# A two-layer recurrent block on one core: the feed-forward's hidden activations in two buffers, its input's split on POOL, its norm two chunks ahead, and another order at its start and at the kernel's end

## The chip, the cores and the metric

The kernel runs on one core of a Trainium2 chip. The metric is the device time of one execution in microseconds. The engines are TensorE (PE in the profile, PEld its weight loads), VectorE (DVE), ScalarE (ACT), GpSimd (POOL) and SyncE (SP), which issues every DMA here. Each engine runs its own list of instructions in order and waits on semaphores for the others.

## What is computed

Four sequences of 1024 tokens, 128 channels. The input is layer-normalised to `xn`. One branch is a block attention on `xn` (16 heads of 8, blocks of 32). The other has two layers of windowed attention and feed-forward. The output is `x + attention * silu(branch)`.

```python
def _layer(x, wqkv, qs, ksc, wo, lg, lb, w1, b1, w2, b2):
    h = shift_token(x)                      # half of the channels come from the token before
    q, k, v = split(h @ wqkv)               # 8 heads of 64, q and k normalised, rotated
    x = x + local_attention(q, k, v) @ wo   # windows of 64, each sees itself and the one before
    h = shift_token(x)
    mu = h.mean(-1, keepdims=True)
    var = h.var(-1, keepdims=True)
    h = (h - mu) / jnp.sqrt(var + 1e-05) * lg + lb
    h = h @ w1 + b1
    a, g = jnp.split(h, 2, axis=-1)         # 341 and 341 columns
    h = a * jax.nn.gelu(g, approximate=False)
    return x + h @ w2 + b2

xn = _layernorm(x)
s = _L0_attn_ref(xn, ...)
for l in range(2): y = _layer(y, ...)       # y starts as xn
out = x + s * silu(y)
```

## The kernel before

Everything lies in SBUF with channels on the partitions; `X` holds all 4096 tokens. The order of each engine is written out by hand, so program order is the schedule. The first phase (to about 165 us) is the input norm and the block attention. Then each of two layers, L0 and L1, has a windowed attention over 32 tiles of 128 tokens (`local(n)` on each engine, tile `n`'s parts spread over several calls), and a feed-forward over 8 chunks of 512 tokens (`ffn(j)` on each engine).

The feed-forward of chunk j is a chain through all engines. PE makes the column mean of the shifted `x` (`mean`, one fp32 matmul), DVE subtracts it (`centre`, writes `D`), ACT squares (`squares`), PE makes the variance (`variance`, one fp32 matmul), ACT takes Ln and Exp(-0.5 ·) (`inverse_deviation`), DVE scales (`scaled`, writes `tA`). The result is split into a high and a low part for three single-pass matmuls: ACT copies it to `split[.., 0, :]` (L954, L972), DVE subtracts that (`lows`, L1253). PE then makes, for each of three parts c of the hidden layer, the gate side and the linear side, 3 matmuls each (`up(c)`: PSUM banks 1 to 6). ACT applies Gelu to the gate side (L949), DVE adds the bias to the linear side and multiplies (`hidden(c)`, L1262, writes `hid`, which lies in the attention's `prob`). PE multiplies by `w2` (three fp32 matmuls into bank 7, the down projection), DVE adds it to `X` (L1274), SP copies the chunk to the shifted buffer `XS` for the next layer.

Before the change `ffn(j)` runs chunk j's `up`, chunk j-1's down projection at the end of the same step, and the norm of chunk j+3. There is one `hid`, so `hidden(0)` of a chunk waits until the down projection of the chunk before is done. On DVE `hidden` of chunk j-1 stands in `ffn(j)`, behind `lows(j+1)`. Gelu, Ln/Exp and Silu need different function tables in ACT, so each step has two table loads, and with L1's Silu in it four. The last layer ends each chunk with Silu (L959), a multiply with the attention's result (L1285) and an add of the input (L1288) on DVE, and a DMA of the chunk.

Between attention and feed-forward, the attention's last tiles (`local(31)` to `local(34)` in the PE list) come first, with the means and variances of chunks 0, 1 and 2 between them; the split of `w1` (L1106, L1108) also stands there on DVE. POOL does nothing in the feed-forward. In the attention it normalises probabilities (L1375) and rotates q and k (L1382 to L1404).

L422 and L432 are the helpers through which every matmul and every transpose goes.

## Time and profile before

| | us |
|---|---|
| median of three runs | 882.16 (880.42 to 882.94) |
| the profiled execution | 883.38 |
| its span, first to last instruction | 881.6 |
| PE busy in it | 787.1 (89%) |
| DVE busy | 682.5 (77%) |
| ACT busy | 669.7 (76%) |
| POOL busy | 531.5 (60%) |
| TensorE clock granted, mean | 0.954 of full |

A time is read against the same execution's span: 1.78 us lie around it. The stages in this span: block attention to about 165 us, L0's windowed attention to about 420, its feed-forward to about 520, L1's windowed attention to about 764, its feed-forward and the output to the end. In the timeline rows a time is a start, the next number a duration, and a bracket tells how long the engine had been idle before and what ended that.

### The profile page before, as it was taken

How to read it: one execution, taken by the hardware profiler on the slowest of the kernel's cores; microseconds unless marked ns; L12 is line 12 of the kernel's file. 1: busy time of each engine (PE TensorE's matmuls, PEld its weight loads, DVE VectorE, ACT ScalarE, POOL GpSimd, SP SyncE). 2: the span in 40 equal slices, each digit the busy share in tenths (PEclk: the TensorE clock that was granted, in tenths of full speed). 3: DMA queues.
4: the chain of work that ended last, by engine and by line, in shares of the span. 5: the costliest groups of instructions: out<-in, count | busy, mean ns of one | idle time of the engine just before them, and what ended most of it. 6: DMA issues, size and time to landing. Idle time of an engine off the chain costs nothing. (4 is left out here: it accounts for less than half of the span.)

```text
span 881.6 us, 26513 instructions
## 1 busy us (share of the span) xinstructions
PE 787.1 (89%) x9720; PEld 595.3 (68%) x9720; DVE 682.5 (77%) x1338; ACT 669.7 (76%) x2041; POOL 531.5 (60%) x505
## 2 busy tenths in 40 slices
PE   4788999878999999999779887999999999878985
PEld 1457777656888888887645545788888888654542
DVE  1577899789999999996234669999999999524455
ACT  2326777549999999998577526999999999747873
POOL 0364334169999999999200007999999999710000
PEclk8899999969999999999899988999999999989996
DMA  9120001002222222222101112222222222212001
GB/s 317 43 49 3 3 4 42 3 19 52 65 65 64 65 64 66 65 65 65 45 19 25 27 34 61 53 65 64 66 65 65 64 65 65 65 31 95 1 36 60
DMA packets 64707, 48.26 MB, mean 55 GB/s; under 512 B 40410, under 2 KB 50948, under 8 KB 64068
## 3 DMA queue, kind: packets, MB, share of 16 engines
q1 hardware_dynamic: 64580, 46.57, 20.9%
...
## 5 line engine op out<-in xcount | busy, mean ns | idle before, releaser
L422 PE MATMUL ps<-wqkv,split 128*128 128x512 f32 x576 | 188.5, 438 | 20.3 <-DVE tA L1157 13.4
L899 ACT ACTIVATE prob<-ps,nmax 128x128 f32<-128x128 f32 x512 | 179.3, 375 | 2.7 <-DVE nmax L1196 2.7
L1382 POOL TENSOR_TENSOR qr<-qr,ss 128x512 f32<-128x512 f32 x64 | 92.0, 1437 | 118.3 <-ACT ss L892 118.3
L1375 POOL TENSOR_TENSOR prob<-prob,rinv 128x512 f32<-128x512 f32 x128 | 133.2, 1042 | 29.1 <-DVE rinv L1203 28.9
L422 PEld LDWEIGHTS ps<-wqkv,split 128*128 128x128 f32 x576 | 98.7, 198 | 35.1 <-issue 25.0
L899 ACT ACTIVATION_READ_ACCUMULATOR prob<-ps,nmax 128x1 f32 x512 | 110.5, 216 | 0.0
L432 PE MATMUL ps<-ident,prob 128*128 128x128 f32 x640 | 97.2, 275 | 9.5 <-POOL prob L1375 9.2
L422 PE MATMUL ps<-split,w 128*128 128x512 f32 (+1 forms) x288 | 87.7, 447 | 15.9 <-DVE prob L1262 14.2
L1196 DVE TENSOR_REDUCE nmax<-ps 128x4 f32<-128x512 f32 x128 | 81.6, 677 | 11.8 <-PE ps L422 11.5
L432 PEld LDWEIGHTS ps<-ident,prob 128*128 128x128 f32 x640 | 76.0, 141 | 21.2 <-POOL prob L1375 13.0
L867 ACT ACTIVATE pT<-ps 128x512 f32<-128x512 f32 x128 | 80.7, 631 | 11.3 <-PE ps L432 11.1
L1390 POOL TENSOR_TENSOR kA<-kn,lrot 128x512 f32<-128x512 f32 x64 | 84.2, 1316 | 0.9 <-DVE kn L1189 0.9
L422 PEld LDWEIGHTS ps<-split,w 128*128 128x128 f32 (+1 forms) x288 | 51.4, 183 | 48.4 <-DVE prob L1262 20.4
L1404 POOL TENSOR_TENSOR kr<-kA,kB 128x512 f32<-128x512 f32 x64 | 81.8, 1277 | 0.3
L422 PE MATMUL ps<-oT,wo 128*128 128x128 f32 x512 | 76.7, 294 | 0.9 <-DVE X L1210 0.9
L1356 POOL TENSOR_TENSOR prob<-D,hmask 128x512 f32<-128x512 f32 x32 | 35.1, 1098 | 59.7 <-PE ps L422 59.6
L422 PE MATMUL ps<-pT,VB 128*64 128x64 f32 x1024 | 67.7, 231 | 3.4 <-issue 3.4
L422 PEld LDWEIGHTS ps<-pT,VB 128*64 128x64 f32 x1024 | 53.1, 140 | 25.8 <-issue 25.8
L422 PEld LDWEIGHTS ps<-oT,wo 128*128 128x128 f32 x512 | 64.3, 197 | 5.8 <-issue 1.5
L422 PE MATMUL ps<-kT,qT 64*64 64x128 f32 x2048 | 67.7, 271 | 0.0
L422 PE MATMUL ps<-pT,V 128*64 128x64 f32 x1024 | 64.7, 225 | 0.0
L422 PEld LDWEIGHTS ps<-kT,qT 64*64 64x64 f32 x2048 | 61.1, 134 | 4.7 <-issue 0.2
(128 smaller groups left out, 1871.8 us busy)
## 6 DMA issues: line engine op xcount, KB each, us to landing
...
XS<-X SPq DMA_DIRECT2D x128, 32.0 KB, 1.9
...
```

The costliest lines, as they stand in the source:

```text
L422: return nc.tensor.matmul(o, l, r, start=start, stop=stop, skip_group_check=True)
L432: return nc.tensor.matmul(o, i, ident[:], is_transpose=True, start=True, stop=True, skip_group_check=True)
L867: nc.scalar.activation(pT[:, grp, :], ps[:, 6, :], ACT.Copy).then_inc(l_pTe[grp], 1)
L899: nc.scalar.activation(prob[:, m % 2, grp, s * P:(s + 1) * P], ps[:, 4 + grp, s * P:(s + 1) * P], ACT.Exp, bias=nmax[:, m % 2, col], accum ...
L1196: v.tensor_reduce(nmax[:, m % 2, 4 * grp:4 * grp + 4], ps[:, 4 + grp, :].rearrange("p (s k) -> p s k", s=4), AX_X, ALU.max, negate=True).t ...
L1356: g.tensor_tensor(kexp[:, par, :].rearrange("p (b h k) -> p b h k", b=BLKS, h=INGRP), part(kR, n, P).rearrange("p (b k) -> p b k", b=BLKS) ...
L1375: g.tensor_tensor(p4, p4, rinv[:, m % 2, 4 * grp:4 * grp + 4].unsqueeze(2).broadcast_to([P, 4, P]), ALU.mult).then_inc(l_prob[grp], 1)
L1382: g.tensor_tensor(hd(qr[:, m % 2, :]), hd(qr[:, m % 2, :]), ss[:, (base + m) % 2, 0:8].unsqueeze(2).broadcast_to([P, HEADS, HD]), ALU.mult ...
L1390: g.tensor_tensor(hd(kA[:]), hd(kn[:]), row8(2, m, 0, HD), ALU.mult)
L1404: g.tensor_tensor(kr[:, m % 2, :], kA[:], kB[:], ALU.add).then_inc(l_kr, 1)
```

## The change

- The hidden activations have two buffers: parts 0 and 1 of chunk j in `prob[:, j % 2]`, part 2 in a slice of `vexp`. The waits for the down projection go one chunk further back.
- The high and low parts of the normalised input are made on POOL (`norm_high`, `norm_low`) from `tA` and `tB` in turn. The copy on ACT and the subtraction on DVE are gone.
- The norm runs two chunks ahead, all in bank 0. A step is on PE `mean(j+2)`, `up(j,0)`, `variance(j+2)`, `down(j-1)`, `up(j,1)`, `up(j,2)`; the three `hidden` of chunk j stand in step j.
- The change-over from attention to feed-forward is written out: the last four tiles' operations and chunk 0's steps are interleaved. `w1`'s split moves into the attention, around `local(20)`.
- L1's Silus stand in two batches, five between chunk 6 and chunk 7 and the rest behind chunk 7. POOL does multiply and add for chunks 0 to 4, DVE for 5 to 7, and chunk 7's last steps run in two halves of 256 columns, the second down projection into bank 0.
- In L0 the tables for L1 (`attn_tables`) stand ahead of `ffn(5)` on DVE, the split of the next `wqkv` ahead of `ffn(6)`.

```diff
@@ -293,6 +296,10 @@
 
         def part(t, j, width):
             return t[:, bass.ds(j * width, width)]
+
+        def hid(j, c):
+
+            return prob[:, j % 2, c, :] if c < 2 else hidx[:, j % 2, :]
 
...
+                def down(j, cols=slice(0, CHUNK), bank=7):
+                    wait(pe, x_new, x_before_ffn(L) + j)
+                    if bank == 0:
+                        pe.wait_ge(ln_log, nb + CHUNKS)
+                    for c, (u, n) in enumerate(PARTS):
+                        pe.wait_ge(ffn_hid, NPART * (fb + j) + c + 1)
+                        last = mm(ps[:, bank, cols], w2[0:n, c, :], hid(j, c)[0:n, cols], c == 0, c == NPART - 1)
+                    last.then_inc(ffn_y, 1)
+
+                def ffn(j):
+                    if j + 2 < CHUNKS:
+                        mean(j + 2)
+                    pe.wait_ge(ffn_lo, fb + j + 1)
+                    up(j, 0)
+                    if j + 2 < CHUNKS:
+                        variance(j + 2)
+                    down(j - 1)
+                    up(j, 1)
+                    up(j, 2)
 
...
+                mean(0)
+                local(TILES - 2, 0)
+                variance(0)
+                local(TILES - 1, 1)
+                mean(1)
+                local(TILES, 0)
+                variance(1)
-                local(TILES, 0)
-                bias_products()
+                pe.wait_ge(w1_made, 1 + L)
+                pe.wait_ge(ffn_lo, fb + 1)
+                up(0, 0)
                 local(TILES + 1, 1)
+                mean(2)
                 local(TILES + 2, 0)
-                variance(2, 2, 0)
                 pe.wait_ge(bias_made, 1 + L)
-                steps(0, CHUNKS - 1 if L + 1 < DEPTH else CHUNKS, ffn)
-                return ffn
+                up(0, 1)
+                variance(2)
+                pe.wait_ge(l_exp[1], 4 * (base + TILES))
+                pe.wait_ge(l_pTe[0], base + TILES)
+                pe.wait_ge(l_pTe[1], base + TILES)
+                up(0, 2)
+                for j in range(1, CHUNKS):
+                    ffn(j)
+                if L + 1 == DEPTH:
+                    for h in range(2):
+                        down(CHUNKS - 1, slice(h * CHUNK // 2, (h + 1) * CHUNK // 2), (7, 0)[h])
+
+                def last_down(j, par):
+                    down(CHUNKS - 1)
+                return last_down
 
...
+                def ffn(j):
+                    if j + 2 < CHUNKS:
+                        squares(j + 2)
+                    gelu(j, 0)
+                    if j + 2 < CHUNKS:
+                        load_exp_and_ln()
+                        inverse_deviation(j + 2)
+                    gelu(j, 1)
+                    gelu(j, 2)
+
+                def silu(j, cols):
+                    x = X[:, bass.ds(j * CHUNK + cols.start, cols.stop - cols.start)]
+                    nc.scalar.activation(x, x, ACT.Silu).then_inc(gate_silu, 1)
+
+                squares(0)
+                local(TILES - 2, 0)
+                probs_copied(TILES - 3, 1)
                 act.wait_ge(l_trq, base + TILES)
-                for j in range(3):
-                    inverse_deviation(j, j)
-                for j, t in enumerate((tA, tB)):
-                    act.wait_ge(ln_scaled, fb + j + 1)
-                    nc.scalar.activation(split[:, j, 0, :], t[:], ACT.Copy).then_inc(ffn_hi, 1)
+                inverse_deviation(0)
+                exponentials(TILES - 1, 0)
+                exponentials(TILES - 1, 1)
+                probs_copied(TILES - 2, 0)
+                o_copied(TILES - 3)
+                probs_copied(TILES - 2, 1)
+                squares(1)
+                probs_copied(TILES - 1, 0)
+                o_copied(TILES - 2)
+                inverse_deviation(1)
                 act.wait_ge(bias_made, 1 + L)
-                if L + 1 < DEPTH:
-                    steps(0, CHUNKS - 1, ffn)
-                else:
-                    steps(0, CHUNKS + 2, ffn)
+                gelu(0, 0)
+                probs_copied(TILES - 1, 1)
+                o_copied(TILES - 1)
+                squares(2)
+                load_exp_and_ln()
+                inverse_deviation(2)
+                gelu(0, 1)
+                gelu(0, 2)
+                for j in range(1, CHUNKS):
+                    ffn(j)
+                    if L + 1 == DEPTH and j == CHUNKS - 2:
+                        for k in range(GATE_POOL):
+                            act.wait_ge(x_new, x_before_ffn(L) + k + 1)
+                            silu(k, slice(0, CHUNK))
+                if L + 1 == DEPTH:
+                    for k in range(GATE_POOL, CHUNKS - 1):
+                        act.wait_ge(x_new, x_before_ffn(L) + k + 1)
+                        silu(k, slice(0, CHUNK))
+                    for h in range(2):
+                        act.wait_ge(x_new, x_before_ffn(L) + CHUNKS + h)
+                        silu(CHUNKS - 1, slice(h * CHUNK // 2, (h + 1) * CHUNK // 2))
 
...
-                steps(0, TILES - 2, local)
+                steps(0, 19, local)
+                ffn_weights_hi(L)
+                local(20, 0)
+                ffn_weights_lo(L)
+                steps(21, TILES - 3, local)
 
...
+                def ffn(j):
+                    if j + 2 < CHUNKS:
+                        norm_centre(j + 2)
+                    hidden(j, 0)
+                    summed(j - 1)
+                    if j + 2 < CHUNKS:
+                        scaled(j + 2)
+                    hidden(j, 1)
+                    hidden(j, 2)
+
+                norm_centre(0)
+                local(TILES - 2, 0)
+                inverse_sums(TILES - 3, 1)
+                inverse_sums(TILES - 2, 0)
+                inverse_sums(TILES - 2, 1)
+                v_copied(TILES - 1)
+                maxima(TILES - 1, 0)
+                maxima(TILES - 1, 1)
+                scaled(0)
+                added_to_x(TILES - 4)
+                inverse_sums(TILES - 1, 0)
+                norm_centre(1)
+                inverse_sums(TILES - 1, 1)
+                added_to_x(TILES - 3)
                 ffn_bias(L)
-                local(TILES + 1, 1)
-
-                def scaled(j, t):
-                    dve.wait_ge(ln_rstd, nb + j + 1)
-                    v.tensor_tensor(t[:], part(D, j, CHUNK), rstd[:, j, :], ALU.mult).then_inc(ln_scaled, 1)
-
-                local(TILES + 2, 0)
-                scaled(0, tA)
-                scaled(1, tB)
-                lows(0, 0, tA)
-                lows(1, 1, tB)
-                dve.wait_ge(bias_made, 1 + L)
-                if L + 1 < DEPTH:
-                    steps(0, CHUNKS - 3, ffn)
-
-                    attn_tables(L + 1, 0)
-                    attn_tables(L + 1, 1)
-                    ffn(CHUNKS - 2, 0)
-                    attn_hi(L + 1)
-                    attn_lo(L + 1)
-                    ffn(CHUNKS - 1, 1)
-                else:
-                    for j in range(CHUNKS + 4):
-                        ffn(j, j % 2)
-                return ffn
+                scaled(1)
+                hidden(0, 0)
+                added_to_x(TILES - 2)
+                norm_centre(2)
+                added_to_x(TILES - 1)
+                scaled(2)
+                hidden(0, 1)
+                hidden(0, 2)
+                for j in range(1, CHUNKS):
+                    if not gate and j == CHUNKS - 3:
+                        attn_tables(L + 1, 0)
+                        attn_tables(L + 1, 1)
+                    if not gate and j == CHUNKS - 2:
+                        attn_hi(L + 1)
+                        attn_lo(L + 1)
+                    ffn(j)
+                if gate:
+                    for k in range(GATE_POOL, CHUNKS - 2):
+                        gated(k, slice(0, CHUNK), k)
+                    gated(CHUNKS - 2, slice(0, CHUNK), CHUNKS - 2)
+                    for h in range(2):
+                        cols = slice(h * CHUNK // 2, (h + 1) * CHUNK // 2)
+                        summed(CHUNKS - 1, cols, (7, 0)[h], h)
+                        gated(CHUNKS - 1, cols, CHUNKS - 1 + h)
+
+                def tail(j, par):
+                    if j == CHUNKS + 1:
+                        summed(CHUNKS - 1)
+                return tail
...
+
+                fb = L * CHUNKS
+
+                def norm_high(j):
+                    pool.wait_ge(ln_scaled, fb + j + 1)
+                    wait(pool, ffn_a, (NPART * (fb + j - 1)) if j > 1 else 0)
+                    g.tensor_copy(split[:, j % 2, 0, :], (tA, tB)[j % 2][:]).then_inc(ffn_hi, 1)
+
+                def norm_low(j):
+                    pool.wait_ge(ffn_hi, fb + j + 1)
+                    g.tensor_tensor(split[:, j % 2, 1, :], (tA, tB)[j % 2][:], split[:, j % 2, 0, :].bitcast(F32),
+                                    ALU.subtract).then_inc(ffn_lo, 1)
+
+                pool.wait_ge(l_v, base + TILES)
+                for j in range(CHUNKS):
+                    norm_high(j)
+                    norm_low(j)
+                if L + 1 == DEPTH:
+                    pool.wait_ge(gate_x, 32)
+                    for j in range(GATE_POOL):
+                        s, x = part(A_OUT, j, CHUNK), part(x_in, j, CHUNK)
+                        pool.wait_ge(gate_silu, j + 1)
+                        g.tensor_tensor(s, s, part(X, j, CHUNK), ALU.mult).then_inc(gate_pool, 1)
+                        pool.wait_ge(gate_pool, j + 1)
+                        g.tensor_tensor(x, x, s, ALU.add).then_inc(gate_first, 1)
 
 
```

The number of table loads in ACT's list goes from 33 to 31.

What stands on ACT, from chunk 7's predecessor to the end of the kernel, before (L949 is Gelu, L954 the copy to the high part, L959 Silu, L765 the load of the Exp and Ln table):

```order
L949 ACT_TABLE_LOAD
L949 ACTIVATE kA<-ps,bias 128x512
L949 ACTIVATE kB<-ps,bias 128x512
L949 ACTIVATE kn<-ps,bias 85x512
L959 ACT_TABLE_LOAD
L959 ACTIVATE X<-X 128x512
L949 ACT_TABLE_LOAD
L949 ACTIVATE kA<-ps,bias 128x512
L949 ACTIVATE kB<-ps,bias 128x512
L949 ACTIVATE kn<-ps,bias 85x512
L959 ACT_TABLE_LOAD
L959 ACTIVATE X<-X 128x512 x4
```

and now (L971 is Gelu, L986 Silu):

```order
L971 ACTIVATE kA<-ps,bias 128x512
L971 ACTIVATE kB<-ps,bias 128x512
L971 ACTIVATE kn<-ps,bias 85x512
L986 ACT_TABLE_LOAD
L986 ACTIVATE X<-X 128x512 x5
L971 ACT_TABLE_LOAD
L971 ACTIVATE kA<-ps,bias 128x512
L971 ACTIVATE kB<-ps,bias 128x512
L971 ACTIVATE kn<-ps,bias 85x512
L986 ACT_TABLE_LOAD
L986 ACTIVATE X<-X 128x512 x2
L986 ACTIVATE X<-X 128x256 x2
```

The Silus stood one to a chunk, each with its table load, and stand in two batches, one of them between the Gelus of chunks 6 and 7.

What stands on DVE between L0's attention and its feed-forward, from the `w1` split on, before (L987 is `centre`, L1203 the inverse of the softmax sums, L1210 the attention's addition to `X`, L1302 `scaled`, L1253 `lows`):

```order
L1106 TENSOR_SCALAR w<-raw,vecs 128x682
L1108 SCALAR_TENSOR_TENSOR w<-raw,vecs,w 128x682
L987 TENSOR_TENSOR D<-XS,ps 128x512
L1117 TENSOR_TENSOR bias<-ps,b 128x2x2
L1118 TENSOR_TENSOR bias<-ps,b 85x2
L1203 RECIPROCAL rinv<-rsum 128x4
L1210 TENSOR_TENSOR X<-X,ps 128x128 x2
L1302 TENSOR_TENSOR tA<-D,qr 128x512
L1302 TENSOR_TENSOR tB<-D,qr 128x512
L1253 TENSOR_TENSOR split<-tA,split 128x512
L1253 TENSOR_TENSOR split<-tB,split 128x512
L987 TENSOR_TENSOR D<-XS,ps 128x512
```

and now, from the first `centre` on (L1033 `centre`, L1251 the inverse sums, L1199 the copy of v, L1244 the maxima, L1258 the addition to `X`, L1308 `scaled`):

```order
L1033 TENSOR_TENSOR D<-XS,ps 128x512
L1251 RECIPROCAL rinv<-rsum 128x4 x2
L1199 COPY V<-ps 128x512
L1244 TENSOR_REDUCE nmax<-ps 128x4 x2
L1258 TENSOR_TENSOR X<-X,ps 128x128
L1251 RECIPROCAL rinv<-rsum 128x4 x3
L1199 COPY V<-ps 128x512
L1244 TENSOR_REDUCE nmax<-ps 128x4 x2
L1308 TENSOR_TENSOR tA<-D,qr 128x512
L1258 TENSOR_TENSOR X<-X,ps 128x128
L1251 RECIPROCAL rinv<-rsum 128x4
L1033 TENSOR_TENSOR D<-XS,ps 128x512
```

The `w1` split is not there any more, `scaled` for chunk 0 stands ahead of the last tiles' inverse sums, and the first `centre` stands ahead of the inverse sums of tiles 28 and 29.

What stands on DVE in one step of L0's feed-forward, before (L1279 is `scaled`, L1262 `hidden`, L1274 the addition to `X`):

```order
L1253 TENSOR_TENSOR split<-tA,split 128x512
L1262 SCALAR_TENSOR_TENSOR prob<-ps,bias,kA 128x512
L987 TENSOR_TENSOR D<-XS,ps 128x512
L1262 SCALAR_TENSOR_TENSOR prob<-ps,bias,kB 128x512
L1262 SCALAR_TENSOR_TENSOR prob<-ps,bias,kn 85x512
L1274 SCALAR_TENSOR_TENSOR X<-ps,vecs,X 128x512
L1279 TENSOR_TENSOR tA<-D,qr 128x512
```

and now (L1315 is `hidden`, L1321 the addition to `X`):

```order
L1033 TENSOR_TENSOR D<-XS,ps 128x512
L1315 SCALAR_TENSOR_TENSOR prob<-ps,bias,kA 128x512
L1321 SCALAR_TENSOR_TENSOR X<-ps,vecs,X 128x512
L1308 TENSOR_TENSOR tA<-D,qr 128x512
L1315 SCALAR_TENSOR_TENSOR prob<-ps,bias,kB 128x512
L1315 SCALAR_TENSOR_TENSOR vexp<-ps,bias,kn 85x512
```

`lows` has gone from the head of the step, `centre` stands first, and the `hidden` of parts 1 and 2 stand last.

## Rows read from the trace of the kernel before

**Rows 1.** Windows: PE, PEld, DVE, ACT, POOL busy; PEclk; DMA share; GB/s.

```profile
600.00:700.00 100.00, 100.00 (x1348) 83.09 (x1343) 99.58 (x205) 96.40 (x357) 99.98 (x95) 1.00 0.27 63
...
764.53:793.37 28.84, 21.18 (x213) 15.90 (x212) 8.93 (x23) 14.88 (x37) 5.12 (x5) 0.88 0.17 40
793.37:813.57 20.20, 15.93 (x54) 9.31 (x54) 6.98 (x12) 15.21 (x19) 0.00 (x0) 1.00 0.28 104
```

**Rows 2.** Timeline of PE, two steps of L1's feed-forward.

```profile
813.57 2.39 PE L422 MATMUL ps<-split,w 128*128 128x512 f32 x9 [0.34 <-DVE prob L1262]
...
818.04 2.74 PE L422 MATMUL ps<-prob,w 128*128 128x512 f32 x6
820.62 1.02 PE L422 MATMUL ps<-XS,mean_w 128*128 128x512 f32 x2
...
822.68 2.39 PE L422 MATMUL ps<-split,w 128*128 128x512 f32 x9 [0.34 <-DVE prob L1262]
```

**Rows 3.** Timeline of ACT and DVE, the same steps.

```profile
814.14 0.63 ACT L929 ACTIVATE sq<-D 128x512 f32<-128x512 f32 x1 [2.09 <-DVE D L987]
...
816.00 1.28 ACT L765 ACT_TABLE_LOAD   x1
...
820.55 0.62 ACT L954 ACTIVATE split<-tA 128x512 fp32r<-128x512 f32 x1
...
821.27 0.69 DVE L1253 TENSOR_TENSOR split<-tA,split 128x512 fp32r<-128x512 f32 x1 [4.59 <-ACT split L954]
```

**Rows 4.** Timeline of PE and POOL, change-over in L1.

```profile
775.87 0.34 PE L422 MATMUL ps<-pT,VB 128*64 128x64 f32 x4 [0.84 <-issue]
...
780.79 1.04 POOL L1375 TENSOR_TENSOR prob<-prob,rinv 128x512 f32<-128x512 f32 x1 [6.68 <-DVE rinv L1203]
```

**Rows 5.** Timeline of PE, L0's feed-forward and the first projections of L1.

```profile
457.49 3.53 PE L422 MATMUL ps<-split,w 128*128 128x512 f32 x9 [2.82 <-DVE prob L1262]
...
466.55:485.93 19.38, 18.70 (x61) 10.52 (x60) 10.20 (x17) 13.87 (x18) 0.00 (x0) 1.00 0.12 27
...
507.23 2.74 PE L422 MATMUL ps<-prob,w 128*128 128x512 f32 x6
509.40 5.18 PE L422 MATMUL ps<-split,w 128*128 128x512 f32 x18
...
521.75 2.90 PE L422 MATMUL ps<-wqkv,split 128*128 128x512 f32 x6 [3.88 <-DVE tA L1157]
```

**Rows 6.** Timeline of DVE, L0's feed-forward: tables for L1, and `hidden` of chunk 7.

```profile
500.26 0.69 DVE L1079 TENSOR_TENSOR lrot<-ltab,scales 128x512 f32<-128x512 f32 x1
...
502.80 0.75 DVE L1262 SCALAR_TENSOR_TENSOR prob<-ps,bias,kA 128x512 f32<-128x512 f32 x1
...
517.20 0.75 DVE L1262 SCALAR_TENSOR_TENSOR prob<-ps,bias,kA 128x512 f32<-128x512 f32 x1 [3.55 <-PE ps L422]
```

**Rows 7.** Timeline of PE, ACT and DVE, the end of L1.

```profile
843.59 5.29 PE L422 MATMUL ps<-split,w 128*128 128x512 f32 x15 [3.89 <-DVE prob L1262]
...
858.25 5.18 PE L422 MATMUL ps<-split,w 128*128 128x512 f32 x18
...
868.82 5.49 PE L422 MATMUL ps<-prob,w 128*128 128x512 f32 x6 [2.81 <-DVE X L1274]
...
864.76 1.15 ACT L959 ACTIVATE X<-X 128x512 f32<-128x512 f32 x2
...
878.39 0.69 DVE L1288 TENSOR_TENSOR XS<-XS,A_OUT 128x512 f32<-128x512 f32 x1
```

**Rows 8.** Sources: shortest, median, longest ns of one, over the whole trace.

```profile
L1142 DVE TENSOR_TENSOR split<-XS,split x64: 285/1126/1128, 169.7 to 729.0; 128x128 fp32r<-128x128 f32 x64
...
L1404 POOL TENSOR_TENSOR kr<-kA,kB x64: 1261/1277/1295, 186.5 to 762.6; 128x512 f32<-128x512 f32 x64
```

**Rows 9.** Groups of DVE instructions by form: busy, mean ns; the `w1` split.

```profile
L1106 DVE TENSOR_SCALAR w<-raw,vecs 128x682 fp32r<-128x682 f32 x2 | 1.1, 571 | 0.0
...
L1108 DVE SCALAR_TENSOR_TENSOR w<-raw,vecs,w 128x682 fp32r<-128x682 f32 x2 | 1.9, 930 | 0.1
```

190 lines of the change are left out of this document (70 added, 120 removed).

## The prediction

> **What bounds the kernel now.** I read the share of each engine by windows first. In the middle of an attention PE, DVE and POOL are each busy 99.6% or more [rows 1]: nothing there is idle. The change-over and the feed-forward are different. From L1's first means to its first feed-forward matmul PE is busy 21.2 of 28.8 us, at a clock of 0.88, and in the next stretch, up to its third step, 15.9 of 20.2 us [rows 1]. This change works there.
>
> Then the timeline of a step. In L1 it repeats every 9.11 us (813.57 to 822.68), and PE shows only 0.34 us of idle in it, waiting for DVE's `hidden` [rows 2]. So PE needs 8.77 us. But PE is not what sets the period: ACT starts its squares after 2.09 us of waiting for `centre`, works without a gap to the end of its copy, and DVE, idle for 4.59 us, waits for that copy, then does `lows`, `hidden`, `centre` [rows 3]. That is a ring of 7.03 us on ACT (814.14 to 821.17) and 2.08 on DVE, 9.11 together. PE has almost the same length by chance. So a change that only breaks the ring finds PE 0.34 us below.
>
> Last the two ends. In L1 the Silus and their tables leave PE idle for 3.89 us ahead of chunk 5's second half; the last `up` starts at 858.25, the last down projection takes 5.49 us where the same six records take 2.74 in a step, and DVE ends at 879.08 (878.39 plus 0.69) [rows 2, 7]. In L0, `hidden` of chunk 7 waits 3.55 us for the down projection of chunk 6, since `hid` is one buffer, and L1's second projection starts at 521.75 after 3.88 us [rows 5, 6].
>
> **The step.** In the new step PE does the same work. What could hold it is the norm's piece: mean, `centre`, squares, variance, now all within one step with only `up(j,0)` between. From the mean's start: mean ready at 1.02 [rows 2], `centre` 0.68 (as long as a `tA` product, 0.69 [rows 3]) to 1.75, squares 0.63 to 2.41 [rows 3], so variance at 2.46. PE has the mean (0.86, half of two overlapping records and a bit) and six matmuls of some 0.245 to fill 2.33 of that: 0.13 us open. `hidden` of part 2 of the chunk before ends near 0.96 and does not delay `centre`. ACT has 6.4 us in 8.8 (7.03 less the copy), DVE 3.9 (4.52 less `lows`) [rows 3], POOL two operations of some 1.3 [rows 8]. I take 8.8 us a step, between 8.77 and 9.11. Steps 6 and 7 have no norm: 2.17 for the down projection (507.23 to 509.40) and 5.0 for the 18 matmuls (5.18 [rows 5]), 7.2 us.
>
> At one place a page speaks against this. Between ACT's Gelu and the next table load the row shows no gap, and 1.28 us for the load itself [rows 3]. The Trainium skill, "ScalarE: Activation LUTs", section "What ACT_TABLE_LOAD costs", adds a drain of about 1.38 us to each switch. By that, ACT would need some 9.2 us for a step with two loads, eight steps would be 0.4 longer and the sum 3 us higher; the trace disagrees, since two loads already fit in ACT's 7.03 us.
>
> **The change-over.** I walked the four engines' new lists with the durations of before. To the second half of `up(2,0)`, before has 7.66 us of PE idle in the first window and 4.27 in the second, 3.4 lost to the clock (12% of 28.8), and by then one more mean and variance, 1.5 us, since it works three chunks ahead: 16.8 us that could go [rows 1]. The waits that replace them, in order: the copy of the turned probabilities of tile 30 now stands behind all eight exponentials of tile 31 on ACT, PE waits 1.1; the values wait for the copy after it, 0.84 as before [rows 4]; the last copy stands behind `gelu(0,0)` with its table load (1.28 + 0.69), 1.6; `up(0,1)` waits for the last addition to `X`, 0.5; and variance(3) waits for `centre(3)`, which stands on DVE behind both last `hidden` of chunk 0, which wait for Ln, Exp, a load and two Gelus: 2.5. Together 6.5. POOL's part is in time: it waited 6.68 us for an inverse sum that stood behind the `w1` split [rows 4]; now its last one ends near 774, its two split operations near 776.5, and PE wants them at 778.9. **Gain in L1 up to step 2: 10.2 us** (803.4 for 813.57). Steps 2 to 5: 26.4 for 30.0 us (843.59 less 813.57), most of it the 3.89 us of Silu; to the last `up`: 0.3. So `up(7,0)` starts at 844.2 for 858.25 [rows 7]: **14.1 us**.
>
> **L0.** The same walk, 346.9 us earlier, puts the third step's `up` at 455.4 for 466.55, 11.2 us, one more than in L1, since PE ran slowly after its 2.82 us of idle: 3.53 us for nine matmuls where 2.39 is usual [rows 2, 5]. From there to `up(7,0)` before has 42.85 us (to 509.40). The change has four steps of 8.8, one of 7.2 and one cost of its own: the tables for L1, 2.54 us on DVE (500.26 to 502.80 [rows 6]), now stand ahead of `centre(7)`, so variance(7) comes 2.35 later, where before they delayed only a `hidden`. That is 44.3, a loss of 1.4. The crossing to L1 gives 0.6: `hidden` of chunk 7 no longer waits, but the first input splits of L1 now follow it, so PE waits 1.4 us for them, then runs one projection, one square on ACT and the q products, 4.5 us in all after chunk 7's `up`. **L0: 10.4 us.**
>
> **The end.** From `up(7,0)` to DVE's end before has 20.83 us [rows 7]. In the new order ACT does a load and five Silus between chunks 6 and 7 (two take 1.15, so five 2.7 [rows 7]), the Gelus of chunk 7 end at about 7.2 us, PE's last matmul at 9.9, the two Silus of chunks 5 and 6 at 9.7. DVE then has four full and four half SBUF-to-SBUF operations, two additions and two waits for a Silu: 15.2 us in all if it is alone. It isn't: POOL is busy with ten operations of about 1.28 us [rows 8] from 1.9 to about 16. A DVE operation of two SBUF inputs beside POOL: 1126 ns median for 285 at the shortest [rows 8], so it waits some 0.84 us. Four full operations and some of the half ones wait so: 19.2 us in all. I take 19, gain **1.8 us**, between 5.6 and 0.
>
> **What it costs.** The `w1` split, 0.57 and 0.93 us [rows 9], stood where DVE waited for others. In the attention nothing is idle [rows 1], so 1.5 a layer is lost at the least; the most is 0.84 more of waiting for each, 3.2 a layer [rows 8]. Nearest to what DVE shows there is the middle, 2.0, so 4.0 us for two layers. And new waits of 1.6 to 2.5 us in the change-over may drop the clock: after 2.82 us of idle nine matmuls took 1.1 more [rows 5], after 3.89 us fifteen took 5.29 [rows 7]. I take 1.25 a layer, 2.5, from 0 to 5.
>
> **Sum** against the profiled execution: 14.1 + 10.4 + 1.8 - 4.0 - 2.5 = 19.8, 883.4 - 19.8 = 863.6. The median of before lies 1.2 us under its profiled execution, so some of that may come off; I give 863.
>
> **Rivals.**
> A. The change-over keeps more waits than I found. Four engines in order, five waits found by hand; one more per layer of the size of the largest (2.5), or an ACT copy or Gelu one place later for each tile, costs 3 to 5 us a layer. For it: PE's gains there are two thirds of the sum. Against: the walk with its waits adds up with the idle time of before. 863.6 + 8 = 871.6.
> B. The port. A DVE operation with two SBUF inputs waits for POOL's whole operation and POOL for it. Then the `w1` split costs 3.2 a layer (2.4 more in all), the first `centre` moved ahead of two inverse sums holds POOL in its full stretch, and the end takes 20.8: 863.6 + 2.4 + 1.8 = 867.8. For it: the median of 1126 ns. Against: rows show whole waits only for small operations. The Trainium skill, "SBUF — State Buffer", section "SBUF: two separate sides", says so: the pair shared by VectorE and GpSimd is an exclusive lock, held for the full instruction. The trace's rows agree in size.
> C. Slower than before. The pause ahead of each variance, small but at the same place of every step, and the five of the change-over keep the clock at its lower level of 1.2 GHz. The last down projection shows what that costs: 5.49 for 2.74 [rows 2, 7]. A step would take about 8 us more; three of the 14 steps would eat the 19.8 us. With five: 863.6 + 40 = 904. Against: pauses of 0.34 in every step left the clock at full in the second window of rows 1.
> D. The ring moves instead of breaking: ACT's and DVE's step stays at 9.1 and POOL's split comes late. Then eight steps give 0.3 less each and the ends less: 863.6 + 2.4 + 3 = 869.
>
> **How the numbers follow.** Forecast 0.62 (857 to 868), A 0.16, B 0.1, D 0.06, C 0.06. What is left out at the top is C and half of A; at the bottom the costs can be 5 us less and the end 3.8 us better, 855. The range is 855 to 872. About 0.3% (2.6 us) is what a measurement of this kernel can tell from no change; below 879.5 is faster: all of the forecast, A, B and D nearly whole, 0.93; within 0.3% 0.02; slower 0.05.
>
> **What the new profile would show.** Steps 2 to 5 in L1 with a period of 8.8 and PE idle for 0.1 to 0.2 us ahead of each variance; at 9.1 the ring is still there. `up(7,0)` of L1 starting 42.4 us after the start of step 2's mean. Idle of 2 to 3 us ahead of variance(3) in both layers, and of some 2.4 ahead of variance(7) in L0. POOL's ten last operations ending about 16 us after `up(7,0)`, and DVE's last multiplications near 1.2 us. L1's attention starting 6 to 9 us earlier than before and taking 1.5 to 3 us longer. The prediction is wrong if the stretch from the first mean to step 2 shrinks by less than 6 us, or if the clock in the steps is below full.

## The result and the profile after

The changed kernel takes 860.15 us (median of four runs, 858.55 to 862.52) where the kernel before takes 882.55 on the same chip (880.42 to 883.22). The ratio is 0.9746, with a 95% interval from 0.9726 to 0.9766. It is faster by 22.4 us; the prediction was 863.0, in a range from 855 to 872. The profiled execution took 862.52 us (span 860.5), so the comparison of the two profiled executions gives 20.9 us, where the sum had 19.8.

The steps of L1 first, PE in the timeline: start, duration, engine, line, operation, out<-in; in brackets idle time and what ended it. Line 437 is the matmul helper; `mean_w` marks means (`XS`) and variances (`sq`).

```profile
790.64 1.12 PE L437 MATMUL ps<-sq,mean_w 128*128 128x512 f32 x2 [2.50 <-ACT sq L957]
791.60 1.88 PE L437 MATMUL ps<-prob,w 128*128 128x512 f32 x4
...
796.96 1.02 PE L437 MATMUL ps<-XS,mean_w 128*128 128x512 f32 x2
797.42 1.97 PE L437 MATMUL ps<-split,w 128*128 128x512 f32 x6
799.43 1.12 PE L437 MATMUL ps<-sq,mean_w 128*128 128x512 f32 x2
...
805.74 1.02 PE L437 MATMUL ps<-XS,mean_w 128*128 128x512 f32 x2
...
814.52 1.02 PE L437 MATMUL ps<-XS,mean_w 128*128 128x512 f32 x2
...
835.69 4.78 PE L437 MATMUL ps<-split,w 128*128 128x512 f32 x18
840.31 1.88 PE L437 MATMUL ps<-prob,w 128*128 128x512 f32 x4
```

From mean to mean a step now takes 8.78 us (805.74 to 814.52), where the rows of before repeat at 9.11 [rows 2]. Between six matmuls and variance 0.04 us are open (797.42 plus 1.97, then 799.43). The last six of the 18 matmuls at 835.69 are `up(7,0)`, so it starts near 838.87, where before had 858.25 [rows 7]. The 2.50 us ahead of variance(3) are one of the new waits. The other waits of the change-over, and POOL's one:

```profile
754.48 0.66 PE L447 MATMUL ps<-ident,prob 128*128 128x128 f32 x4 [1.55 <-POOL prob L1437]
...
767.86 0.63 PE L447 MATMUL ps<-ident,prob 128*128 128x128 f32 x4 [0.84 <-ACT pT L895]
769.42 0.34 PE L437 MATMUL ps<-pT,VB 128*64 128x64 f32 x4 [0.93 <-issue]
...
777.60 0.34 PE L437 MATMUL ps<-pT,VB 128*64 128x64 f32 x4 [1.61 <-issue]
...
781.97 1.67 PE L437 MATMUL ps<-split,w 128*128 128x512 f32 x6 [0.38 <-DVE X L1258]
```
```profile
753.38 1.04 POOL L1437 TENSOR_TENSOR prob<-prob,rinv 128x512 f32<-128x512 f32 x1 [1.41 <-DVE rinv L1251]
```

The first of them is not new. The kernel before has a wait of the same length behind its first means:

```profile
767.54 0.66 PE L432 MATMUL ps<-ident,prob 128*128 128x128 f32 x4 [1.55 <-POOL prob L1375]
```

The whole stretches, by windows (us, then busy time of PE, PEld, DVE, ACT, POOL with counts, the granted clock, DMA share, GB/s): the change-over, the steps with a norm, the steps without, the end.

```profile
751.46:782.00 30.54, 25.00 (x314) 19.41 (x312) 10.26 (x27) 20.92 (x62) 16.20 (x17) 1.00 0.22 50
782.00:797.42 15.42, 12.92 (x44) 7.71 (x45) 5.73 (x9) 11.69 (x15) 2.06 (x3) 1.00 0.39 142
797.42:826.20 28.78, 28.60 (x93) 16.36 (x92) 14.10 (x20) 20.48 (x26) 7.44 (x8) 1.00 0.00 1
826.20:838.85 12.65, 12.65 (x44) 7.68 (x43) 5.85 (x8) 7.20 (x10) 1.89 (x2) 1.00 0.00 0
838.85:860.50 21.65, 10.30 (x37) 6.16 (x35) 12.31 (x15) 10.60 (x16) 14.10 (x10) 0.87 0.26 97
```

The window of before from its first means had a granted clock of 0.88 [rows 1]; now it is 1.00 from L1's first mean to the last chunk. The steps are PE's: 28.60 of 28.78 us. What is left of idle in L1 lies in the change-over, 5.5 and 2.5 us.

L0, ahead of variance(7), and the crossing into L1:

```profile
488.17 1.12 PE L437 MATMUL ps<-sq,mean_w 128*128 128x512 f32 x2 [2.49 <-ACT sq L957]
489.14 3.19 PE L437 MATMUL ps<-prob,w 128*128 128x512 f32 x4
492.12 1.45 PE L437 MATMUL ps<-vexp,w 85*128 85x512 f32 x2
...
506.58 3.35 PE L437 MATMUL ps<-split,w 128*128 128x512 f32 x12
511.49 0.94 PE L437 MATMUL ps<-wqkv,split 128*128 128x512 f32 x3 [1.56 <-issue]
514.55 2.90 PE L437 MATMUL ps<-wqkv,split 128*128 128x512 f32 x6 [2.12 <-DVE tA L1205]
```

The wait is the forecast one; behind it four matmuls take 3.19 us instead of 1.88, at a granted clock near half (0.58 from 489.10 to 492.10), the lower of its two levels. The steps of L0 ahead of it run at full clock (1.00 from 436 to 488). L1's second projection starts at 514.55 for 521.75 [rows 5]. In the attention, POOL, which had no gap before, has two in each layer, right behind the parts of the `w1` split on DVE (here L1's):

```profile
677.59 1.04 POOL L1437 TENSOR_TENSOR prob<-prob,rinv 128x512 f32<-128x512 f32 x1 [0.54 <-DVE rinv L1251]
685.89 1.04 POOL L1437 TENSOR_TENSOR prob<-prob,rinv 128x512 f32<-128x512 f32 x1 [0.89 <-DVE rinv L1251]
```

The end, DVE (POOL's ten operations run from 841.16 to 855.65):

```profile
848.21 1.31 DVE L1326 TENSOR_TENSOR A_OUT<-A_OUT,X 128x512 f32<-128x512 f32 x1 [0.31 <-ACT X L986]
849.56 1.63 DVE L1329 TENSOR_TENSOR XS<-XS,A_OUT 128x512 f32<-128x512 f32 x1
851.12 1.74 DVE L1326 TENSOR_TENSOR A_OUT<-A_OUT,X 128x512 f32<-128x512 f32 x1
...
857.73 0.42 DVE L1329 TENSOR_TENSOR XS<-XS,A_OUT 128x256 f32<-128x256 f32 x1
```

### The profile page after: what moved, and what is told of

The parts are those of the page before. It is cut to its first block and busy times, and to the rows that moved or that the text cites. A ratio compares the mean times of both kernels' runs of the same rounds, so it can differ in the third digit from the quotient of the medians.

```text
span 860.5 us, 26521 instructions
## 1 busy us (share of the span) xinstructions
PE 775.0 (90%) x9726; PEld 588.2 (68%) x9726; DVE 677.8 (79%) x1315; ACT 656.3 (76%) x2024; POOL 578.1 (67%) x547
## 3 DMA queue, kind: packets, MB, share of 16 engines
q8 instruction: 79, 1.29, 0.6%
## 5 line engine op out<-in xcount | busy, mean ns | idle before, releaser
L1244 DVE TENSOR_REDUCE nmax<-ps 128x4 f32<-128x512 f32 x128 | 81.6, 677 | 11.0 <-PE ps L437 10.7
L437 PE MATMUL ps<-split,w 128*128 128x512 f32 (+1 forms) x288 | 82.7, 432 | 0.8 <-DVE X L1258 0.8
L437 PE MATMUL ps<-oT,wo 128*128 128x128 f32 x512 | 73.9, 287 | 0.0
L437 PEld LDWEIGHTS ps<-oT,wo 128*128 128x128 f32 x512 | 62.1, 191 | 5.2 <-issue 0.8
L1190 DVE TENSOR_TENSOR split<-XS,split 128x128 fp32r<-128x128 f32 x64 | 64.1, 1001 | 0.2
```

The lines of the kernel that those rows point to most:

```text
L437: return nc.tensor.matmul(o, l, r, start=start, stop=stop, skip_group_check=True)
L1190: v.tensor_tensor(split[:, slot, 1, cols], shifted(XS[0], m, P), split[:, slot, 0, cols].bitcast(F32), ALU.subtract).then_inc(l_split, 1)
L1244: v.tensor_reduce(nmax[:, m % 2, 4 * grp:4 * grp + 4], ps[:, 4 + grp, :].rearrange("p (s k) -> p s k", s=4), AX_X, ALU.max, negate=True).t ...
```

## The experiments

All times below are medians beside runs of the kernel before on the same chip; the ratio's interval is given. The changed kernel stands at 860.15 us and 0.9746 [0.9726, 0.9766]. Of the single moves that make it faster only **ladder** has an interval clear of this one; for the others the reading rests on stretches of the traces, one execution each.

### What the second buffer and POOL are worth

**one_hid**: one buffer of Gelu outputs.

```diff
-            return prob[:, j % 2, c, :] if c < 2 else hidx[:, j % 2, :]
+            return prob[:, 0, c, :] if c < 2 else hidx[:, 0, :]
...
-                    wait(dve, ffn_y, (fb + j - 1) if j > 1 else 0)
+                    wait(dve, ffn_y, (fb + j) if j > 0 else 0)
```

> The changed kernel with one buffer of Gelu outputs again: hidden(j) waits for the down projection of chunk j-1 as in the kernel before. Everything else is the change. Theory (the second buffer is hardly used in the new order, since down(j-1) stands ahead of up(j,1)): only hidden(j,0) comes later, by some 3 us, the summing right after it by 0.7, and nobody waits for either, since up(j,1) and the Gelus wait for banks of part 1 and 2. Steps stay at 8.80 us, idle ahead of hidden(7,1) and down(7) unchanged, time within 0.5 us of the changed kernel's 860.2. Rival (the prediction's reading of the 3.55 us wait of hidden in L0, and of two buffers breaking the ring): at least the 3.55 us of L0's last chunk come back, 863.7 or more, and with the ring some 0.3 us in each of eight steps on top, 866.

861.95 us, 0.9763 [0.9746, 0.9781]. DVE in an L0 step of this kernel:

```profile
465.71 0.69 DVE L1033 TENSOR_TENSOR D<-XS,ps 128x512 f32<-128x512 f32 x1
470.85 0.75 DVE L1315 SCALAR_TENSOR_TENSOR prob<-ps,bias,kA 128x512 f32<-128x512 f32 x1 [4.46 <-PE ps L437]
...
474.49 0.69 DVE L1033 TENSOR_TENSOR D<-XS,ps 128x512 f32<-128x512 f32 x1
```

`hidden(j,0)` does wait, 4.46 us where it waited 1.33, and the step from centring to centring is still 8.78. The theory of the step holds: in the new order the second buffer is worth nothing that the steps show. The time does not settle it as well: it lies 1.8 us above the changed kernel's, between the theory (0.5) and the rival (3.5 or more). The two intervals overlap, and of the two profiled executions this one is the shorter (861.11 against 862.52), so the 1.8 us have no place in the traces.

**parts_back**: high part on ACT ahead of `gelu(j,1)`, low part on DVE behind `scaled`, POOL without them.

```diff
                         inverse_deviation(j + 2)
+                        norm_high(j + 2)
                     gelu(j, 1)
...
                         scaled(j + 2)
+                        norm_low(j + 2)
                     hidden(j, 1)
```

> The changed kernel with the high part of the normalised chunk back on ACT (behind the inverse deviation) and the low part back on DVE (behind the scaling), POOL without them; all other orders as changed. Theory (the ring of ACT and DVE is what the move to POOL breaks): ACT's list from one squares to the next becomes 6.57 us of work, 0.69 of waiting for the scaling, 0.63 of copy, and hidden(j,2) 0.75 and the centring 0.69 on DVE, 9.3 us, over PE's 8.78. So steps with a norm take 9.3 instead of 8.80, 5 to 6 of them a layer, and PE idles 0.5 more ahead of each variance: 5 to 6 us in all, and up to 1 a layer more in the change-over: 865 to 868. Rival (PE sets the step whatever the others do, and the gain of the step came from the order on PE): steps stay at 8.8, time 860 to 861.

913.73 us, 1.0348 [1.0327, 1.0369], slower than the kernel before: the theory missed by 46 to 49 us, the rival by 53. ACT and PE in an L0 step:

```profile
468.16 0.63 ACT L965 ACTIVATE qr<-lnlog 128x512 f32<-128x512 f32 x1
473.90 0.63 ACT L970 ACTIVATE split<-tA 128x512 fp32r<-128x512 f32 x1 [5.11 <-PE ps L437]
474.55 1.28 ACT L976 ACT_TABLE_LOAD   x1
475.84 0.69 ACT L976 ACTIVATE kB<-ps,bias 128x512 f32<-128x512 f32 x1
```
```profile
479.33 1.26 PE L437 MATMUL ps<-sq,mean_w 128*128 128x512 f32 x2 [3.28 <-ACT sq L957]
480.39 3.48 PE L437 MATMUL ps<-prob,w 128*128 128x512 f32 x4
```

My count of ACT's work had left out the copy's own wait. `split` has two buffers, and chunk j+2 goes where `up(j,2)` is still reading, so the copy waits 5.11 us and two Gelus stand behind it. PE then idles 3.28 us a step and runs the next matmuls at the low clock: 13.7 us a step (DVE's `tA` at 471.71, `tB` at 485.44).

**parts_back2**: the same, the copy behind `gelu(j,2)`, the subtraction behind the next centring.

```diff
                     gelu(j, 1)
                     gelu(j, 2)
+                    if j + 2 < CHUNKS:
+                        norm_high(j + 2)
```

> As parts_back (high part on ACT, low part on DVE), but with the copy of chunk j+2 behind the last Gelu of chunk j instead of ahead of its second one, and the subtraction behind the next centring. In parts_back the copy waited 5.11 us for up(j,2), which still read the same buffer, and two Gelus stood behind it. Theory A (what POOL is worth is a queue in which nobody stands behind that wait; the 0.63 us of copy and the 0.69 of subtraction are nothing): here the copy is asked for after up(j,2) has ended and runs while DVE centres, so steps with a norm take 8.8 us, and only the first copies in the change-over cost something, 0 to 1.5 us a layer: 860 to 863. Theory B (the copy's time itself is in the ring, as the prediction read it): steps take 8.8 + 0.3 to 0.6, and the time is 864 to 869.

864.02 us, 0.9786 [0.9760, 0.9811]; the profiled execution, the fastest of the four, took 861.32. Its steps take 8.78 us (means at 804.26 and 813.04) and its waits are those of the changed kernel, but for 0.69 instead of 0.38 ahead of `up(0,1)`. By its median it lies in theory B's range, 3.9 us above the changed kernel; the steps speak for theory A, since B had them at 9.1 or more. Both of its change-overs ran partly at the low clock (3.43 and 3.46 us for four matmuls behind variance(3)), 1.7 us each, which the changed kernel's did not. **orders_only** puts both together, one buffer and no parts on POOL. What stays of the change is the orders, the batches of Silus, POOL's multiplications and additions for chunks 0 to 4, and the halves of chunk 7:

> The changed kernel with one buffer of Gelu outputs and with the high and low parts on ACT and DVE (each copy behind the last Gelu, as in parts_back2): of the change only the orders are left, norm two chunks ahead, the interleaved change-over, w1's split in the attention, batched Silus, drain. Theory (the time is won by the order of the work, and the second buffer and POOL are worth 0 to 4 us together, as the two single runs had it): 861 to 865, steps at 8.8 us. Rival (each of the two alone can be missed because the other covers for it: with one buffer hidden(j,0) waits 4.5 us for the down projection, and the copy and the subtraction then stand behind it, so the ring closes): steps of 9.1 or more, 869 or more.

861.09 us, 0.9761 [0.9737, 0.9785]; steps of 8.80 (803.68 to 812.48). So nearly all of the 22 us comes without the second buffer and without the split on POOL; together they are worth 0.9 us by the medians, and the two intervals leave room for anything from nothing to some 4 us. How the 22 us divide among what stays is read from the stretches before and after: no run takes back the order of the change-over, the batches of Silus or POOL's part in the end.

### What the new costs are worth

**w1_back**: both halves of the `w1` split behind the last inverse sum of the change-over.

```diff
-                ffn_weights_hi(L)
-                local(20, 0)
-                ffn_weights_lo(L)
...
                 inverse_sums(TILES - 1, 1)
+                ffn_weights_hi(L)
+                ffn_weights_lo(L)
```

> The changed kernel with both parts of the split of w1 out of the attention's tiles, behind the last inverse sum of the change-over (DVE sat idle for 3.87 us there). Theory (in the attention POOL is full and waits 0.54 and 0.90 us for the inverse sums that stand behind the two parts): POOL's two waits in each attention go, each attention is 1.43 us shorter, the change-over is unchanged since DVE is idle there and up(0,0) wants w1 six us later: 2.9 us faster, 857.3. Rival 1 (POOL and DVE hold each other up there, so that the 1.7 us of DVE's work delays the last normalise, the last splits and up(0,0)): half or more of it comes back, 859 to 862. Rival 2 (the attention catches up on its own what POOL loses): no change, 860.

859.36 us (854.59 to 859.98), 0.9722 [0.9692, 0.9752]. POOL's two gaps are gone in both attentions. From L1's fourth q projection to its first mean the kernel takes 220.97 us (527.68 to 748.65), where eight of the nine kernels tried here that keep the split there take 222.0 to 222.2 (parts_back 222.8): 1.1 us. The change-over of L1 takes 36.16 us from the first to the last of its waits (751.66 to 787.82), as in the changed kernel (754.48 to 790.64). But L0's does not: same waits, yet

```profile
430.17 1.95 PE L437 MATMUL ps<-oT,wo 128*128 128x128 f32 x8
...
451.10 1.13 PE L437 MATMUL ps<-sq,mean_w 128*128 128x512 f32 x2 [2.50 <-ACT sq L957]
452.06 3.35 PE L437 MATMUL ps<-prob,w 128*128 128x512 f32 x4
```

Four matmuls take 3.35 us for 1.88, and eight take 1.95 for 1.16 twenty us before: the lower clock took back 3.2 us (48.74 us from the first mean to step 2's mean, 45.50 in the changed kernel). So the gaps and L1's stretch put the price of the split at 1.1 to 1.4 us a layer. The median, 0.8 us less, does not show the 2.9 us of the theory, and taken alone it lies nearer to rival 2; one run of four (854.59) is faster than the theory.

**tables**: the tables and the `wqkv` split for L1 behind `hidden(j,0)` of steps 2 to 5.

```diff
                     hidden(j, 0)
+                    if not gate and j == 2:
+                        attn_hi(L + 1)
+                    if not gate and j == 3:
+                        attn_lo(L + 1)
+                    if not gate and 4 <= j <= 5:
+                        attn_tables(L + 1, j - 4)
...
-                    if not gate and j == CHUNKS - 3:
-                        attn_tables(L + 1, 0)
-                        attn_tables(L + 1, 1)
-                    if not gate and j == CHUNKS - 2:
-                        attn_hi(L + 1)
-                        attn_lo(L + 1)
```

> The changed kernel with the tables and the wqkv split for L1 spread over DVE's idle stretches in L0's steps 2 to 5, behind hidden(j,0), instead of standing in a row ahead of chunk 7's centring and of step 6. Theory (the 2.49 us that PE waits for variance(7) in L0, and the low clock after it, 3.19 us for four matmuls instead of 1.88, come from the tables alone): centring(7) follows hidden(5,2) at once, PE's idle ahead of variance(7) is 0.1 to 0.2, the matmuls behind it take 1.88 again: 2.4 + 1.9 = 4.3 us faster, 855.9. Rival (the clock falls there or a little later for another reason, such as the low activity around the layer's end): only 2.4 us, 857.8, with slow matmuls still behind variance(7) or moved to the crossing. A third: DVE's idle stretches are short of 0.3 us for the low part of wqkv, so one scaling comes late, and costs 0.3 to 1 us of the gain.

855.70 us, 0.9704 [0.9674, 0.9735]. From step 2's first `up` to the last twelve matmuls of chunk 7, L0 takes 45.32 us for 49.44 (457.19 to 502.51; 457.14 to 506.58): 4.1, both the wait and the slow matmuls gone, as the theory had it. Only the wait comes from the tables for certain: in w1_back, parts_back2, orders_only and silus the same wait of 2.48 or 2.49 us stands ahead of variance(7), and the four matmuls behind it take 1.88. DVE's `L1136` took 1.75 us here and 2.71 in the changed kernel, where it ran beside POOL.

**ladder**: four places of the change-over.

```diff
+                inverse_sums(TILES - 4, 1)
+                inverse_sums(TILES - 3, 0)
                 norm_centre(0)
-                local(TILES - 2, 0)
+                v_copied(TILES - 2)
...
-                gelu(0, 0)
                 probs_copied(TILES - 1, 1)
                 o_copied(TILES - 1)
+                gelu(0, 0)
...
-                hidden(0, 0)
                 added_to_x(TILES - 2)
                 norm_centre(2)
                 added_to_x(TILES - 1)
+                hidden(0, 0)
                 scaled(2)
+                norm_centre(3)
                 hidden(0, 1)
```

> The changed kernel with four places of each change-over in another order: the centring of chunk 0 behind the inverse sums of tiles 28 and 29 (POOL waited 1.41 us for them); the copies of the last turned probabilities and of the last outputs ahead of gelu(0,0) with its table load (PE waited 1.61), and hidden(0,0) behind the additions to X; the centring of chunk 3 ahead of hidden(0,1) and (0,2) (PE waited 2.50 ahead of variance(3)). Theory (each of these waits is the one that ends last at its place): they shrink by 1.4, 1.1 and 1.4, so mean of chunk 4 comes 3.9 us earlier after the first mean in each layer, 7.8 in all: 852.4, and a granted clock that is no worse. Rival 1 (the next wait stands close behind, as in a chain of four engines): half of it, 856. Rival 2 (the clock: other pauses at other times let it fall in a change-over, as it did in three of four runs of the kernel with w1's split moved, at 1.6 and 1.7 us): 0 to 3.3 us of the gain lost, with PE's rows at twice their length somewhere between the first mean and step 2.

852.20 us, 0.9646 [0.9626, 0.9667]. From the first mean to step 2's mean 41.72 us for 45.50 in L1 (746.00 to 787.72; 751.46 to 796.96). Each wait shrank: 1.55 is no longer listed, 1.61 became 0.92, 2.50 became 0.89. That is 3.8 us, where 3.9 was expected. In L0 the waits shrink as much (to 0.89 and 0.90), but the same stretch takes 43.30 us for 45.50, only 2.2 less: the clock fell in the middle of it, where the changed kernel's had not. The last section has the rows. So rival 2 came true in one layer of this execution; the medians differ by 7.95 us, where 7.8 was expected.

**cross**: the last down projection of L0 ahead of L1's second q projection.

```diff
-                    steps(-3, -2, local)
+                    local(-3, 1)
                     tail(CHUNKS, 0)
+                    local(-2, 0)
```

> The changed kernel with the last down projection of L0 on PE ahead of the second q projection of L1 instead of behind it and the k projection. Theory (PE idles 2.12 us ahead of the second q projection for DVE's q products, and all that the down projection needs, hidden(7,2), is done 0.7 us before that idle starts): the down projection, 2.7 us at full clock and 4 at the low one as now, fills the idle; L1's second q projection starts up to 0.6 us later but everything behind it 2 to 3 us earlier: 857.5. Rival (ACT's square of k and DVE's products set the ramp of L1's attention, and PE's order there is free): the third q projection comes at the same time as before, no change, 860. A second rival: which of DVE's and POOL's operations comes first in the ramp changes, worth 1.1 us either way, as between two runs with the same order there.

858.73 us, 0.9724 [0.9709, 0.9739]. From L0's last twelve `up` matmuls to L1's fourth q projection it takes 19.33 us (505.49 to 524.82), where **tables** takes 20.39 (502.51 to 522.90); the changed kernel's 21.61 holds 1.2 us of another kind, told of in the last section. So 1.1 us, less than the 2 to 3 expected: the next wait for `tA` grew from 2.12 to 2.71 us. The median is 1.4 us under the changed kernel's, within the two intervals.

### The end

**gate3**: three chunks gated on POOL instead of five (`GATE_POOL = 3`).

> The changed kernel with three chunks gated on POOL instead of five, and so three Silus between chunks 6 and 7 and four chunks, fully, on DVE behind the last hidden. Theory (DVE's operations of two inputs in the buffer take 1.31 to 1.74 us each only because POOL works beside them, and some 0.65 alone): POOL ends about when DVE begins, ACT's gelu(7,0) comes 1.1 us earlier, DVE's eight full operations take 5.4 us in place of 6.3 for four; DVE ends some 2 us earlier: 858. Rival (these operations take 1.3 us or more by themselves): eight take 11 to 12 us, the end comes 4 us later, 864.

859.13 us, 0.9725 [0.9708, 0.9742]. DVE, with POOL's last operation at 842.63:

```profile
842.75 1.71 DVE L1326 TENSOR_TENSOR A_OUT<-A_OUT,X 128x512 f32<-128x512 f32 x1 [0.97 <-ACT X L986]
844.49 0.69 DVE L1329 TENSOR_TENSOR XS<-XS,A_OUT 128x512 f32<-128x512 f32 x1
845.10 0.68 DVE L1326 TENSOR_TENSOR A_OUT<-A_OUT,X 128x512 f32<-128x512 f32 x1
```

Beside POOL 1.71 us, the same operation alone 0.68: POOL's runs to 843.91, 1.16 us behind the start of DVE's. Eight full operations take as long (6.3 us) as four beside POOL. The theory on the port is right; its sum was not, since the first operation still ran beside POOL and waited 0.97 for a Silu: from chunk 6's down projection to DVE's end 17.5 us for 17.8. The median is 1.0 us under the changed kernel's, within the two intervals.

**silus**: the five Silus behind `gelu(6,0)` instead of `gelu(6,2)`, and both halves of chunk 7 summed ahead of the gating of chunk 6.

> The changed kernel with the batch of five Silus and its two table loads behind gelu(6,0) instead of behind gelu(6,2), and on DVE both summings of chunk 7 ahead of the gating of chunk 6. Theory (the end is set by POOL's ten operations and DVE's, which hold each other up: a DVE operation took 0.68 alone and 1.31 to 1.74 beside POOL; the batch delays POOL's start by the time of chunk 6's Gelus): the batch fits into ACT's 3.28 us of idle ahead of gelu(6,1) but for 2 us that nobody waits for; POOL starts 4.9 us earlier and is done about 2 us after DVE's last hidden, so DVE's later operations take 0.68 again: the end comes 4 us earlier, 856. Rival 1 (PE's last down projection sets the end, since the last Gelu can't come before up(7,2) ends, only 0.4 us earlier than now): 859.5. Rival 2 (gelu(6,1) and (6,2) come so late that up(7,1) waits for their banks): no gain or 1 us of loss, with PE idle ahead of up(7,1).

857.25 us, 0.9718 [0.9693, 0.9744]. DVE:

```profile
845.41 1.61 DVE L1326 TENSOR_TENSOR A_OUT<-A_OUT,X 128x512 f32<-128x512 f32 x1 [1.12 <-ACT X L990]
...
851.02 0.42 DVE L1329 TENSOR_TENSOR XS<-XS,A_OUT 128x256 f32<-128x256 f32 x1
```

From chunk 6's down projection (837.88) to DVE's end 13.6 us for 17.8: 4.3 us, as expected. PE has no wait from there to its end, so rival 2 falls; its last down projection ends only 1.2 us earlier behind chunk 6's (8.5 us for 9.7) while the end comes 4.3 earlier, so rival 1 falls too. The run moves the Silus and the two summings at once, and what each is worth is not separated. The median gains 2.9, not 4: in its profiled execution both change-overs ran at the low clock behind variance(3) (3.27 and 3.18 us for four matmuls).

### All together

**best5** has all five moves, and the first two input splits of L1 inside L0's last chunk; **best4** has four chunks on POOL.

```diff
                     hidden(j, 0)
+                    if not gate and j == CHUNKS - 1:
+                        next_inputs(L + 1)
                     summed(j - 1)
```

> All moves together: w1's split in the change-over, tables and wqkv split spread over L0's steps, the four places of the change-over, the down projection of L0's last chunk ahead of L1's second q projection, the Silus behind gelu(6,0) with both summings earlier, and new: the first two input splits of L1 ahead of L0's last hidden, where DVE idles 1.7 us (PE waited 1.56 us for them). If each wait is its own and they add up: 2.9 + 4.1 + 7.6 + 1.1 + 4 + 1.2 = 20.9 less than 860.2, 839.3. If the moves share their gains (the crossing's two moves fill the same idle of PE; with fewer pauses elsewhere the clock falls in other places) some 4 to 6 us of that are missing, 844. If the clock falls in each change-over at 1.6 us a time as in some of the other runs, 847.

> As best5, with four chunks gated on POOL and one more on DVE. By the lock (1.28 us of POOL for what DVE does in 0.68) the end has 1.2 us less work, and ACT's batch is 0.55 shorter: 1 us faster than best5. Against it: DVE's list behind the last hidden is two operations longer, and if POOL has already ended by then nothing is saved there: up to 1.3 us slower than best5.

best5: 839.63 us, 0.9515 [0.9501, 0.9529]; best4: 840.18, 0.9517 [0.9504, 0.9530], no difference. Both beat the changed kernel by some 20 us, nearly as much as that beats the one before, and best5 meets the sum of the expected gains (839.3). The gains measured one by one add up to less by their medians: 0.8, 4.5, 7.9, 1.4 and 2.9 are 17.5 of 20.5 us, and the sixth move had no run of its own. By stretches of the two profiled executions, in us:

| | changed | best5 |
|---|---|---|
| to L0's first mean | 411.18 | 409.32 |
| L0's change-over, first mean to step 2's mean | 45.50 | 43.36 |
| to the last twelve `up` matmuls of L0 | 49.90 | 45.72 |
| crossing, to L1's fourth q projection | 21.61 | 17.94 |
| L1's attention, to its first mean | 223.27 | 222.09 |
| L1's change-over | 45.50 | 41.70 |
| steps, to chunk 6's down projection | 43.35 | 43.35 |
| to DVE's end | 17.84 | 13.50 |

The crossing had 19.33 us in **cross**. L0's change-over holds a fall of the clock that costs 1.7 us. The 1.1 us that the `w1` split cost L1's attention in w1_back are not seen here: 222.09 us is what kernels with the split take.

## Why the prediction was right, point by point

**The step.** 8.8 us forecast, 8.78 measured, and 0.04 us open ahead of each variance where 0.13 was worked out. Steps without a norm were sized at 7.2 and take 6.8 (833.52 to 840.31): eighteen matmuls take 4.6 us there, and I had scaled them from a stretch of before that takes 5.02, with 0.14 of pause in it. So `up(7,0)` comes 41.9 us after step 2's mean, not 42.4.

**The change-over.** Five waits forecast at 1.1, 0.84, 1.6, 0.5 and 2.5 us; the trace has 0.84, 0.93, 1.61, 0.38 and 2.50. One was missed, and it is an old one: PE waits 1.55 us for POOL, and POOL 1.41 us for inverse sums that stand on DVE behind `centre(0)`, which itself waits 1.01 us for the mean. The kernel before has the same 1.55 us behind its first means, where two centrings stand ahead of the same inverse sums, and I had counted them among the idle time that goes. Against it, two waits of PE just ahead of the first means of before (0.49 and 0.34 us at 757.07 and 758.07), outside the window that I had counted, are gone. From the second q projection of L1 (7.2 us earlier) to step 2's second half (813.57 before, near 798.2 now, 15.4 earlier) the change gains 8.2; forecast were 10.2 less 2.0 and 1.25, 6.95. With the measured costs of this stretch, 1.43 for the split and 1.2 in the ramp, the change-over itself gave 10.8. With the missed wait and the two that went it should have given 9.5; for the other 1.3 us I have no place, and the whole attention lies in this stretch. In L0 the step behind the change-over starts 9.4 us earlier (457.14 for 466.55), 10.8 with the split; forecast were 11.2. So the size was right in part by luck.

**A sign of being wrong that did appear.** The prediction called itself wrong if the stretch from the first mean to step 2 shrinks by less than 6 us. Taken by its words it shrinks by 3.2 us in L1 (763.67 to 813.57 before, 751.46 to 798.2 now). The sign was badly chosen: the change puts the first mean one tile earlier in the attention. From the last projection of the attention, which both kernels have at the same place, it shrinks by 11.8 us (760.28 to 813.57; 756.69 to 798.2).

**L0.** Forecast for the wait ahead of variance(7) 2.35, measured 2.49; for the second projection 10.4 less 2.0 and 1.25, 7.15, measured 7.2.

**The end.** 19 us forecast from `up(7,0)` to DVE's end, 19.3 measured (838.87 to 858.15). POOL ends 16.8 us after `up(7,0)`, forecast 16. DVE's multiplications took 1.31 and 1.74 us, where I named 1.2.

**The costs.** The `w1` split: 2.0 a layer forecast, 0.54 + 0.90 = 1.44 measured by POOL's gaps, 1.1 by w1_back's L1. It is at or below the lower end of the forecast, because nearly no waiting at the port came on top: DVE's two operations took 0.61 and 1.14 us there, 0.57 and 0.93 in the change-over of before. The clock: 2.5 for two layers forecast, 1.3 + 0.4 in L0 behind variance(7) and nothing in L1's change-over in this execution. What was not in the sum: 1.2 us in the ramp of L1's attention, explained below. Costs 1.9 us lower than forecast, the ramp 1.2 higher, and the stretches together some 0.4 better make the 20.9 for 19.8.

**The reading that does not hold** is that of the reasons. The prediction had the copy on ACT and the subtraction on DVE as parts of the ring, and in L0 `hidden` of chunk 7 waiting 3.55 us because there is one buffer. orders_only has neither the second buffer nor POOL's help and loses next to nothing: the ring is opened with both operations on the engines where they were. On DVE the centring no longer stands behind the subtraction, so ACT's squares no longer wait for ACT's own copy (argued from the lists; that place alone was not tried). Of the move to POOL parts_back shows one worth: not the 0.63 us of ACT's copy but a queue in which nobody stands behind a wait of 5.11 us. parts_back2 gets the same on ACT, by the place of the copy.

**Rivals.** A (more waits in the change-over): one more, 1.55 us of PE a layer, smaller than the rival's 2.5 and inside the forecast's range. B (the port): the mechanism is there at the end, as gate3 shows, but the end had been sized with it, and the `w1` split did not cost its 3.2 us a layer. The first centring holds POOL up as B said, but by its place in DVE's queue and its own wait for PE, not at the port. The Trainium skill's rule ("SBUF — State Buffer", "SBUF: two separate sides") of a lock for the full instruction agrees with 1.71 beside POOL against 0.68 alone. C (the clock low in every step): the windows show 1.00; in step 5 of L0 it did fall, behind the 2.49 us. D (ring moves): steps of 9.1 are not there. By the Trainium skill ("ScalarE: Activation LUTs", "What ACT_TABLE_LOAD costs") a step of two loads would have taken ACT some 9.2 us, an estimate from the page's figure, which the steps of 8.78 exclude; parts_back's rows again show the Gelu 0.01 us behind the end of a 1.28 us load.
